# Causal scores made twice: probabilities written already turned, the layer end one round later in its own PSUM bank, and a new order on four engines

## The reference

```
q, k, v = split_heads(ln(x) @ Wq), ...           # 16 heads of 8 channels
score = where(causal, q @ k.T, -inf) / sqrt(8)   # 256 x 256 for each head
x = x + softmax(score) @ v (heads joined) @ Wo   # this sum is x3 in the kernel
logits = ln(x) @ Wg.T                            # router: softmax over 8 experts, 64 tokens each
```

## Time and profile before

| what | before |
|---|---|
| median of 3 runs (lowest, highest) | 2342.65 us (2340.35, 2346.33) |
| the profiled execution: time, span of its instructions | 2353.02 us, 2351.2 us |
| busy over the span: PE, DVE, ACT, POOL | 74%, 71%, 54%, 54% |
| mean granted clock of TensorE | 0.787 |

### The profile page before, as it was taken

How to read it: one execution, slowest core, us unless ns; L and a number is a source line. 1 busy time by engine, 2 the same in 40 slices (tenths; PEclk the granted TensorE clock), 3 DMA queues, 4 the chain that set the end, 5 groups by cost and what they waited for, 6 DMA issues and landing times. The chain is left out here.

```text
span 2351.2 us, 43046 instructions
## 1 busy us (share of the span) xinstructions
PE 1734.4 (74%) x14047; PEld 1174.6 (50%) x14047; DVE 1674.5 (71%) x3177; ACT 1280.8 (54%) x3078; POOL 1272.7 (54%) x1169
## 2 busy tenths in 40 slices
PE   1267778778778878877887887887787737777495
PEld 0145555555555555555555555555555524554364
DVE  8888888888888888888888889888987511311011
ACT  1256666666666666666666666666666514322131
POOL 4555455455554555555445555554552063778787
PEclk9987777787777777778778778777877857787797
DMA  3001101011010101110110010000000010223233
GB/s 102 19 19 23 23 22 24 20 31 25 22 27 22 22 22 23 24 25 22 24 22 22 22 22 22 22 22 22 22 20 21 17 41 25 36 45 38 47 34 33
DMA packets 211005, 64.69 MB, mean 28 GB/s; under 512 B 147590, under 2 KB 202767, under 8 KB 210960
## 3 DMA queue, kind: packets, MB, share of 16 engines
q1 hardware_dynamic: 188386, 47.31, 8.8%
q0 software_dynamic: 22528, 16.79, 5.4%
q10 hardware_dynamic: 46, 0.00, 0.0%
HBM read 34.70 MB, written 29.36 MB: 27 GB/s over the span
## 5 line engine op out<-in xcount | busy, mean ns | idle before, releaser
L1056 PE MATMUL pb<-ident,arena 128*128 128x128 f32 x1536 | 285.4, 298 | 164.8 <-ACT arena L954 147.8
L497 POOL TENSOR_TENSOR arena<-arena,eps_t 128x2 f32<-128x2 f32 x128 | 46.6, 364 | 604.5 <-DVE arena L802 350.9
L954 ACT ACTIVATE arena<-pb 128x384 f32<-128x384 f32 x512 | 254.8, 498 | 147.3 <-PE pb L1056 109.7
L1056 PEld LDWEIGHTS pb<-ident,arena 128*128 128x128 f32 x1536 | 180.8, 150 | 299.3 <-issue 155.4
L679 POOL TENSOR_TENSOR arena<-state,c_cross 128x448 f32<-128x448 f32 x128 | 180.3, 1429 | 214.4 <-DVE state L558 131.7
L671 POOL TENSOR_TENSOR arena<-arena,neg_half 128x32 f32<-128x32 f32 x64 | 266.5, 4186 | 16.7 <-DVE arena L535 15.6
L946 ACT ACTIVATE arena<-pd,arena 128x128 f32<-128x128 f32 x512 | 190.7, 372 | 143.9 <-DVE arena L834 141.5
L947 ACT ACTIVATE arena<-pd,arena 128x256 f32<-128x256 f32 x512 | 247.3, 483 | 0.0
L1324 DVE TENSOR_TENSOR arena<-pa,arena 128x512 f32<-128x512 f32 x32 | 22.1, 692 | 291.9 <-remote 161.9
L1276 POOL DMA_INDIRECT out_x<-arena x128 | 204.1, 1594 | 47.0 <-issue 35.9
L1338 ACT ACTIVATE arena<-pd,b 128x512 f32<-128x512 f32 x128 | 86.9, 687 | 208.9 <-PE pd L1354 103.1
(11 more groups left out here) (241 smaller groups left out, 4273.6 us busy)
## 6 DMA issues: line engine op xcount, KB each, us to landing
arena<-v_rows_scratch SPq DMA_DIRECT2D x512, 8.0 KB
amps_scratch<-arena SPq DMA_DIRECT2D x32, 256.0 KB, 2.0
arena<-amps_scratch SPq DMA_DIRECT2D x32, 256.0 KB, 3.3
x_land<-in_L_attn_query SPq DMA_DIRECT2D x32, 128.0 KB, 2.1
arena<-in_L_attn_query SPq DMA_DIRECT2D x32, 128.0 KB, 2.2
v_rows_scratch<-arena SPq DMA_DIRECT2D x32, 128.0 KB, 1.7
out_x<-x SPq DMA_DIRECT2D x32, 128.0 KB, 1.8
xn_scratch<-xn_d SPq DMA_DIRECT2D x32, 128.0 KB, 1.9
```

The costliest lines, as they stand in the source:

```text
L954: act.activation(p_t[:, s % 8, :], pb[:, 0:384], ACT.Copy).then_inc(S("b_pt"), 1)
L1056: mm = pe.transpose(pb[:, j * P:j * P + P], p_raw[:, s % 3, j * P:j * P + P], ident[:, :])
```

## The change

Scores are made a second time with keys on partitions (`turned(n)`): the mask, the products of keys and queries, and a product of a matrix of -1 with a row of minima, all summed in one bank, so that ScalarE's exponents come out with keys on partitions, as the values want them. Minima get to a row by two transposes for four heads (`maxima(q)`) and one copy (`n_rows`). The transposes of probabilities, their copies and `p_raw` are gone. Scores use two banks of `pd`, the second scores the other two, the projections borrow one of these, and stage D has `pb` for itself. D of a batch runs a round later (b-4), and the last one stands alone (`LAYER_END`). The copy of `x2` becomes a stage G of its own, and POOL, ACT, PE and DVE get new orders (PE's and DVE's are shown; the others are likewise new).

```
-PE_ORDER = "F1E3F1E1A1E1A1E2F1E1A1E6B1E1B1E7B1E8B1D3B1D2"
+PE_ORDER = "F1A1D1A1E2A1E1F1E1D1F1E1D1E8B1D1E2B1E3D1B1E1B1E2B1E5"
-DVE_ORDER = "C2A1F2A1C5E1C1F2E1C1E1C1F1B2A2E1C1E1C3E1C2B1C1E1B1A4B1E1A1C3A1B1A2D2A1B2D3B3A1D2A2D1A1D1"
+DVE_ORDER = "C1A2C8F1C1F1C1A2D1E1C1F1D1F1C2E1A1F1D2B1E1C1D1C2A1B1E1A1C1A1C1A1E1C1A1E1A2B2E1A1B2D1A1D1B1A1B1E1A1D1B1D1A1B2"
...
         def vector_e(v, b):
             for n in range(NPAIR):
-                s = slice(2 * (n % 2), 2 * (n % 2) + 2)
+                q, s = n // 2, 32 * (SEQ[2 * n] // 4)
...
+                if n % 2 == 0 and not (isinstance(b, int) and b == 0 and q < 2):
+                    v.wait_ge(S("b_nt"), 4 * b + q - 1)
                 v.wait_ge(S("b_s"), NPAIR * b + n + 1)
-                v.tensor_reduce(n_max[:, 0, 2 * n:2 * n + 2], pd[:, s, 0:128], AX, ALU.min)
-                v.tensor_reduce(n_max[:, 1, 2 * n:2 * n + 2], pd[:, s, 128:384], AX, ALU.min).then_inc(S("b_m"), 1)
+                v.tensor_reduce(n_pad[:, q % 2, 0, s:s + 33:32], pd[:, 0:2, 0:128], AX, ALU.min)
+                v.tensor_reduce(n_pad[:, q % 2, 1, s:s + 33:32], pd[:, 0:2, 128:384], AX, ALU.min).then_inc(S("b_m"), 1)
...
-            for s in range(H1N):
-                yield
-                exponents(s)
-                if s:
+            for q in range(4):
+                yield
+                act.wait_ge(S("b_nt"), 4 * b + q + 1)
+                act.activation(n_rows[:, q % 2, :], pd[:, 0, 0:256], ACT.Copy).then_inc(S("b_nr"), 1)
+                for s in range(4 * q, 4 * q + 4):
                     yield
-                    turned(s - 1)
...
+                    if s % 2 == 0:
+                        act.wait_ge(S("b_st"), NPAIR * b + s // 2 + 1)
+                    if s >= 8 and s % 4 == 0:
+                        act.wait_ge(S("b_pv"), 4 * b + q - 1)
+                    act.activation(p_t[:, s % 8, :], pd[:, 2 + s % 2, 0:384], ACT.Exp, scale=-1.0).then_inc(S("b_e"), 1)
...
-            def turn(s):
-                pe.wait_ge(S("b_e"), H1N * b + s + 1)
-                if s:
-                    pe.wait_ge(S("b_pt"), H1N * b + s)
-                for j in range(3):
-                    mm = pe.transpose(pb[:, j * P:j * P + P], p_raw[:, s % 3, j * P:j * P + P], ident[:, :])
-                mm.then_inc(S("b_p_read"), 1)
+            def maxima(q):
+                pe.wait_ge(S("b_m"), NPAIR * b + 2 * q + 2)
+                for t in range(T):
+                    mm = pe.transpose(pd[:, 0, t * P:t * P + P], n_pad[:, q % 2, t, :], ident[:, :])
+                mm.then_inc(S("b_nt"), 1)
+
+            def turned(n):
+                q = n // 2
+                if n == 0:
+                    pe.wait_ge(S("b_qk"), 4 * b + 4)
+                else:
+                    pe.wait_ge(S("b_e"), H1N * b + 2 * n)
+                pe.wait_ge(S("b_nr"), 4 * b + q + 1)
+                heads_of = [(divmod(SEQ[2 * n + i], 4), pd[:, 2 + i, :]) for i in range(2)]
+                for _, o in heads_of:
+                    pe.matmul(on_diagonal(o), ident_b[:, :], mask_kq[:, :, :], start=True, stop=False, skip_group_check=True)
+                for k, (at, to) in enumerate(((slice(0, 2 * P), slice(0, 2 * P)), (slice(P, 2 * P), slice(2 * P, 3 * P)))):
+                    for (g, r), o in heads_of:
+                        rows_of = slice(32 * g, 32 * g + 32)
+                        pe.matmul(o[:, to], k_t[rows_of, k * P:k * P + P], q_m[rows_of, r, at], start=False, stop=False,
+                                  skip_group_check=True)
+                    for (g, r), o in heads_of:
+                        rows_of = slice(32 * g, 32 * g + 32)
+                        mm = pe.matmul(o[:, to], neg_rows[rows_of, :], n_rows[rows_of, q % 2, at], start=False, stop=True,
+                                       skip_group_check=True)
+                mm.then_inc(S("b_st"), 1)
...
-            for s in range(H1N):
-                yield
-                turn(s)
-                if s % 2 and s // 2 + 2 < NPAIR:
+            for q in range(4):
+                yield
+                maxima(q)
+                if q < 3:
                     yield
-                    scores(s // 2 + 2)
-                if s % 4 == 0 and s:
+                    scores(2 * q + 2)
+                if q:
                     yield
-                    values(s // 4 - 1)
+                    values(q - 1)
+                yield
+                turned(2 * q)
+                if q < 3:
+                    yield
+                    scores(2 * q + 3)
+                yield
+                turned(2 * q + 1)
...
-                together(eng, stages, {"A": b, "C": b - 1, "F": b - 2, "B": b - 2, "E": b - 3, "D": b - 3}, order)
+                together(eng, stages, {"A": b, "C": b - 1, "F": b - 2, "B": b - 2, "E": b - 3, "G": b - 3, "D": b - 4}, order)
```

More of the change, by code:

```diff
@@ L194, in build @@
         x1 = first("x1", [P, T, E])
+        n_pad = first("n_pad", [P, 2, T, P])
+        neg_rows = first("neg_rows", [P, P])
+        mask_kq = first("mask_kq", [P, 2, P], BF16)
         state = sb("state", [P, 2, T, 2, E])
@@ L223, in build @@
         v_sums = [v_slots[:, :, 2 * c:2 * c + 6:5, DK] for c in range(2)]
-        n_max = first("n_max", [P, T, H1N])
-        p_raw = first("p_raw", [P, 3, 3 * P])
+        n_rows = first("n_rows", [P, 2, T * P])
         p_t = first("p_t", [P, 8, 3 * P])
@@ L1023, in tensor_e @@
             for k in range(2):
[L1024 removed]
+                pe.matmul(pd[:, 2, k * 256:k * 256 + 256], w_l1[:, k * P:k * P + P], xnt_e[:, :], start=True, stop=True)
             for t in range(T):
@@ L1034, in scores @@
                     pe.wait_ge(S("b_qk"), 4 * b + n // 2 + 1)
-                if n == 1 and not (isinstance(b, int) and b == 0):
-                    pe.wait_ge(S("b_roff"), b)
-                if n >= 2:
-                    pe.wait_ge(S("b_e"), H1N * b + 2 * n - 2)
-                heads_of = [(divmod(SEQ[2 * n + i], 4), pd[:, 2 * (n % 2) + i, :]) for i in range(2)]
+                    if n:
+                        pe.wait_ge(S("b_nr"), 4 * b + n // 2)
+                else:
+                    pe.wait_ge(S("b_m"), NPAIR * b + n)
+                heads_of = [(divmod(SEQ[2 * n + i], 4), pd[:, i, :]) for i in range(2)]
                 for _, o in heads_of:
@@ L1090, in tensor_d @@
             pe.wait_ge(S("b_oraw"), b + 1)
+            if not (isinstance(b, int) and b == 0):
+                pe.wait_ge(S("b_roff"), b)
             for k in range(2 * T):
-                mm = pe.transpose(pd[:, 3, k * P:k * P + P], o_raw[:, k * P:k * P + P], ident[:, :])
+                mm = pe.transpose(pb[:, k * P:k * P + P], o_raw[:, k * P:k * P + P], ident[:, :])
             mm.then_inc(S("b_o9"), 1)
@@ L1349, in up @@
                 for f in range(NF):
-                    if g == 0 and e == 0 and f == 3:
-                        pe.wait_ge(S("b_roff"), B)
                     if e:
@@ L1407, in pieces_of @@
         def pieces_of(order):
-            runs = order.replace("A", " A").replace("B", " B").replace("C", " C").replace("D", " D").replace("E", " E").replace("F", " F").replace("S", " S").split()
+            runs = order.replace("A", " A").replace("B", " B").replace("C", " C").replace("D", " D").replace("E", " E").replace("F", " F").replace("G", " G").replace("S", " S").split()
             return "".join(r[0] * int(r[1:]) for r in runs)
@@ L1451, in _ @@
             load_experts(sp)
-            for b in range(1, 3):
+            for b in range(1, 4):
                 load_x(sp, b + 1)
                 send(sp, b - 1)
-                if b == 2:
+                if b > 1:
                     load_x0(sp, b - 1)
-            with sp.Fori(3, B - 1) as b:
+            with sp.Fori(4, B - 1) as b:
                 load_x(sp, b + 1)
                 send(sp, b - 1)
-                sync_d(sp, b - 3)
+                sync_d(sp, b - 4)
                 load_x0(sp, b - 1)
@@ L1463, in _ @@
                 send(sp, b - 1)
-                sync_d(sp, b - 3)
+                sync_d(sp, b - 4)
                 load_x0(sp, b - 1)
-            for b in range(B - 2, B):
+            for b in range(B - 3, B):
                 sync_d(sp, b)
```

83 lines of the change are left out of this document (38 added, 45 removed).

## The result

The changed kernel takes 2493.5 us in the median of four runs (2439.4 to 2542.8), the kernel before 2342.6. Two of the four lay over 1.5% above the fastest and are left out of the comparison: the ratio is **1.048 (95% interval 1.043 to 1.053), slower**. The profiled execution, the only one with a trace, took 2475.1 us. The forecast was 2325, with 2400 as the upper end.

The account below looks back on a forecast made before the run. VectorE was taken to set today's pace, TensorE to pace from the third pair of scores: 22.5 + 1.9 + 27.9 + 2.0 + 1.4 = 55.7 us a round; 29 x -0.8 and +4 gave 2325 us (2305 to 2340; outer 2260 to 2400).

Parts of the forecast that it names:

- 27.9: TensorE's stretch from the third pair of scores to the down projection: 26.9 us of work, plus the late row of minima.
- the forecast change of the span, -19: Whole kernel: 29 rounds at -0.8 us each, -23, and +4 for the last batch.
- TensorE's clock is low where it counts: Rival, slower: idle time ahead of the dense stretch leaves TensorE at 1.2 GHz into it; 2375 at 5 us; chance 0.28.
- its far case: Clock rival with 9 us of the dense stretch at the lower level: round 59.5 us, total 2434.
- The rest of the round: Path of one loop round, through VectorE, a hand-over and TensorE: 55.7 us, range 55.1 to 56.2, against 56.5 before.
- The second scores of a pair: TensorE's added mask and products of both widths: 2.02 us a pair at the upper clock level, between 1.17 and 4.04.
- the second tanh: On ScalarE behind two table loads of 1.28 us; VectorE and then TensorE wait about 0.7 us a round.
- The last batch: Stage E alone, paced by TensorE at 25.5 us instead of ScalarE at 21.6: +4 us.
- the start: Two more masks at the start of the kernel, taken at nothing.
- the 23 us that the rounds were to gain: 29 rounds with the old stage E in full, each 0.8 us shorter.
- The rivals on code: TensorE's longer loop no longer stays loaded, so each round fetches code, 1.7 to 5 us: 2375 to 2470; chance 0.04.
- VectorE's floor: VectorE without waits needs 50.2 us a round; rival that second scores overlap more: 2160 at best, 2260 halfway; chance 0.12.

Follow-up runs that it names:

- Runs 1, 2 and 3: run 1, run 2, and five runs of the changed kernel with unused ScalarE copies ahead of the copy of the row of minima: 2354 to 2795 us.
- run 1: Changed kernel with each round's second row of minima transposed into bank pb, so the next scores need not wait for ScalarE's copy: 2276.0 us.
- run 2: Changed kernel with all its waits, plus 7 and 4 unused transposes behind the second and third row of minima: 2326.7 us.
- the run without the subtraction: Against run 1, the products subtracting minima from the second scores left out and the exponents scaled instead: 2215.4 us.
- The run with a stop of 1.24 us: Changed kernel with one unused ScalarE copy ahead of the copy of the second row of minima: 2354 to 2383 us.
- six copies: Changed kernel with six unused ScalarE copies ahead of the copy of the second row of minima, a 2.63 us stop: 2760 to 2763 us.

## Why the prediction was wrong, point by point

**The step that failed** is this one: "Once, the row of minima comes 0.95 us late, since its copy stands behind two exponents: 27.9." The wait is there, at the place named, and measures 0.97 us. But it was priced by its length alone. In 9 of 31 rounds the clock falls there, in one more, the first, 18 us ahead of the stop, and these ten rounds are 16.1 us longer than the others (70.1 against 54.0), 161 us in all. Runs 1, 2 and 3 show this: without the stop, or with it filled, 2276 and 2327; made 1.5 us or longer, 2667 to 2795. The distance from the forecast change of the span, -19, to the measured +122 is 161 for the long rounds, 32 for the two ends of the kernel and 5 for the experts, less 57 by which the rounds were otherwise shorter than forecast.

**The rival "TensorE's clock is low where it counts"** named the resource, not the place or the size. It looked at the idle time ahead of the dense stretch, took 9 us at the lower level as its far case, and 59.5 us for the round. The stretch is 37.5 us and the round 70.1. I read the earlier trace rows, with 0.56 in the half of the round that stops between steps, as the price of long idle places, and did not ask what a single stop inside a dense stretch does.

**The rest of the round held, and came out shorter.** Forecast 55.7 (55.1 to 56.2), measured 54.0 where the clock holds, below the range. The second scores of a pair take 1.83 us at 2.4 GHz (849.39 to 851.22 in the rows above) where 2.02 was forecast, 1.5 us a round. VectorE is busy 48.3 (forecast 49.0), TensorE 47.5 at 0.91 in the short round (45, above 0.9). VectorE's waits for the layer end's first transposes, 46.0 us before, are 17.0 us in the last two batches and none in the loop. Had all rounds been short, the profiled run would have taken 161 us less, 2314; run 2, with its rounds of 54.6, takes 2327.

**Mis-sized terms.** VectorE waits 79.1 us in 22 rounds for the three tanh of a round (L918), but that mean mixes two kinds: 1.8 us in a short round, of which 1.2 for the second tanh behind its table loads, where I took 0.7, and 9.6 in a long one. Its second longest wait, for scores (L1043), is 1.6 and 7.0 in the two rounds shown. Both grow with the long rounds and do not cause them. ScalarE is busy 607.5 / 22 = 27.6 us a round, not 25; it is no bound. The last batch costs 21.1 us more, not 4: I priced it at 2.4 GHz, and its first 74 us run at a granted 0.54. With the stop gone (run 1) it still costs 94.5 - 80.6 = 13.9. How much of this is the clock stays open, since before the clock was low there too. Nothing was set down for the start, and the first projection comes 14.9 us later, in every version of the changed kernel. These two ends alone, 32 us more than forecast, would have used up the 23 us that the rounds were to gain.

**The rivals on code and VectorE's floor.** q8 carried 31 packets instead of 27, but none between 478.5 and 1748.3 us, where only q1 has packets: the longer loop of TensorE stays loaded. No version reached VectorE's floor of 50.2 in the loop; the closest is the run without the subtraction, 51.2.

## What to carry to other kernels

Price a stop of TensorE in the middle of a dense stretch by what lies behind it at half speed, not by its length: 0.97 us here cost 16 in nine of 31 rounds. Look for such stops where a product waits for its bank to be emptied by an engine that has other work in its queue, and give that result a bank of its own, or put unused full-size products into the gap. When a change is to be judged, fill the stops of the kernel before as well, or the clock is judged in place of the change.

## What the hardware showed unexpectedly

The clock's two levels make two round lengths out of one program: 54.0 and 70.1 us, the same instructions, a stop of the same 0.97 us. A fallen clock could stay down while TensorE worked nearly without a stop (36.6 of 37.2 us busy at 0.50); in these rounds it came back behind the down projection, a gate and up projection or a burst of full-size transposes, all of them on 128 rows. The run with a stop of 1.24 us has 1 long round of 31, where 0.97 has 10 and 1.52 has 27. In every run the lengths of the loop's rounds settle into a pattern that nearly repeats: one length (run 2), two in turn (run 1) or five (six copies). The Trainium skill (TensorE: Matmul & The Clock Gate, A second HAM failure mode: psum-queue depth-cycling) tells of a kernel in which small idles between groups of products make the clock swing between its levels; the trace agrees, with one stop of 0.97 us a round as enough. Why 0.97 us tips some rounds and not others stays open.
